# Weighing two units in one run: where the loop of a field-interaction kernel turns

## The chip, the cores and the metric

One core of a Trainium2 chip runs the whole kernel. The time is that of the device for one execution, in microseconds (us); lower is better. TensorE multiplies, VectorE forms products, ScalarE copies, GpSimd (POOL) and SyncE (SP) set up and issue transfers.

## The reference

```python
def _cin_forward(x, Ws):
    x0 = x
    h = x
    outs = []
    for W in Ws:
        h = jnp.einsum('bid,bjd,ijh->bhd', x0, h, W)
        outs.append(h)
    out = jnp.concatenate(outs, axis=1)
    return out.sum(axis=-1)
```

x has 512 rows of 39 fields of 64 numbers, W0 is 39 x 39 x 128 and W1 is 39 x 128 x 128; all of it is float32. The result is 512 x 256: for each row the sums over the 64 numbers of both layers' 128 outputs. The kernel uses that the last sum runs over d: products of fields can be summed first and weighed with the (combined) weights afterwards.

## The kernel before, in words

A setup multiplies W1 by W0 into combined weights and sorts them into lists (`c0`, `c1`); it ends at about 95 us and isn't touched by the change.

After it the 512 rows are 256 pairs of rows. A **unit** is 8 pairs, a **four** is 4 of them, and a **batch** is 64 pairs, 8 units. There are 4 batches. For each unit:

- SP loads `x_w` (the windows, 360 KB, L301) and `x_d` (the listed fields, 448 KB, L308), each into one of two buffers. The order of SP's queue is x_d of unit u, then x_w of unit u, and so on. x_w of u waits until TensorE has done the sums of u-2; x_d of u waits until products and singles of u-2 are done.
- VectorE forms the unit's products in one of two buffers (L413 to L422), after the sums of unit u-2 have read it. ScalarE adds 10 single columns to each list (`singles`, L509).
- TensorE sums (L614): 96 matmuls for each four, in 4-byte floats and so with two passes each where one stands in the code, 64 rows by 32 columns of weights. A four fills two PSUM banks; four banks are used in turn, so four q waits until ScalarE has emptied the banks of four q-2.
- ScalarE empties the banks (L557), two copies for a four, into the batch's slots `s0`: 115 slots of 128 x 128.

The slots of a finished batch are **weighed** during the next batch: a slot is multiplied with its weights and added to `out_ps` (L630, 26 matmul records for 13 slots). ScalarE first stages the slots, because they lie in the arena with the batch's rows spread: 13 slots for each unit, in two halves of 6 and 7 slots (L541), in one staging buffer `t_0`. Half h may be staged when half h-2 has been weighed. The last 11 slots of a batch (the rest, `REST_HALVES`) are staged and weighed after its eighth unit; then ScalarE takes the result out of PSUM (`take_out`, L532), and TensorE starts the next with `begin_out` (L625). The fourth batch is weighed at the very end in one run of 230 matmuls.

TensorE runs loops: the body of the inner one is a **turn** of two units, one for each buffer, and it turns four times in a batch. ScalarE, VectorE and SP run straight lists of instructions. Before a unit's sums TensorE's sequencer waits for windows, products and singles (L653), and before each four for its banks (L658). For weighing it waits for a staged half (L678), and calculates addresses by register instructions.

Of the kernel before, what the change touches and what calls it, by code (L numbers as in the profile page):

```python
# [28 lines left out]
LISTED = 115  # L29
SINGLES = 10  # L30
# [71 lines left out]
def cin_kernel(nc: bass.Bass, x_w: bass.AP, x_d: bass.AP, w0: bass.AP, w1: bass.AP, c1: bass.AP, out: bass.AP):  # L102
# [3 lines left out]
    PAIRS = 64  # L106
    UNIT = 8
    FOUR = 4
    BATCHES = ALL_PAIRS // PAIRS
    UNITS = ALL_PAIRS // UNIT  # L110
    FOURS = ALL_PAIRS // FOUR
    B = 2 * PAIRS
    BANK = 512
    PROD = 4 * LISTED
    PRODS, WS, DS = 2, 2, 2

    IN_BATCH = PAIRS // UNIT
    EACH = PAIRED // IN_BATCH
    HALVES = [(0, EACH // 2), (EACH // 2, EACH)]
    REST = LISTED - IN_BATCH * EACH  # L120
    REST_HALVES = [(0, EACH // 2), (EACH // 2, REST)]
# [4 lines left out]
    with ctx:  # L126
        def sem(name):
            return ctx.enter_context(nc.semaphore(name))
# [10 lines left out]
        def view(start, *dims, rows=(0, P)):  # L139

            ap = [[WORDS, rows[1] - rows[0]]] + [[step, count] for step, count in dims]
            return bass.AP(arena, rows[0] * WORDS + start, ap)

        c0 = take(PAIRED * HID)
        s0 = [take(LISTED * B)]
# [3 lines left out]
        t_0 = take(EACH * B)  # L149
# [15 lines left out]
        banks = [ctx.enter_context(nc.psum_tensor(f"stage{i}", [P, BANK], F32)) for i in range(6)]  # L165
# [14 lines left out]
        filled = sem("filled")  # L180
        emptied = sem("emptied")
# [4 lines left out]
        staged = sem("staged")  # L186
        weighed = sem("weighed")
# [10 lines left out]
        SETUP_BANKS = Y_BANKS + len(TURNS)  # L198
# [6 lines left out]
        def emptied_through_four(q):  # L205
            return SETUP_BANKS + 2 * (q + 1)
# [297 lines left out]
        @block_.scalar  # L504
        def _(act):
            def singles(u):

                act.wait_ge(d_loaded[u % DS], 16 * (u // DS + 1))
                nc.scalar.copy(view(prod0 + u % PRODS * UNIT * PROD, (PROD, UNIT), (LISTED, 4), (1, SINGLES)),  # L509
                               view(d_0 + u % DS * UNIT * D_WORDS + D_SINGLES, (D_WORDS, UNIT), (SINGLES, 4), (1, SINGLES)))\  # L510
                    .then_inc(singles_ready, 1)

            g = 0
            for f in range(FIELDS):
                for a, b in Y_PARTS:
                    act.wait_ge(filled, g + 1)
                    nc.scalar.copy(view(y0 + f * Y_WIDTH + a, (1, b - a)), banks[g % RING][:, 0:b - a]).then_inc(emptied, 1)  # L517
                    g += 1
            act.wait_ge(z_ready, 1)
            for u in range(PRODS):  # L520
                singles(u)
            for k, n in TURNS:
                act.wait_ge(filled, g + 1)
                nc.scalar.copy(view(c0 + k * HID, (1, n * HID)), banks[g % RING][:, 0:n * HID]).then_inc(emptied, 1)  # L524
                g += 1

            def take_out(n):

                act.wait_ge(weighed, IN_ALL * (n + 1) if n < BATCHES - 1 else IN_ALL * n + 1)
                if n >= 1:  # L530
                    act.wait_ge(out_stored, 16 * n)
                nc.scalar.copy(view(out_sb0, (1, 2 * HID)), out_ps[:, 0:2 * HID]).then_inc(out_free, 1)  # L532
                act.wait_ge(out_free, n + 2)
                act.dma_start(out[n * B:(n + 1) * B, :], view(out_sb0, (1, 2 * HID))).then_inc(out_stored, 16)

            def stage(first, a, b, half):


                if half >= 2:
                    act.wait_ge(weighed, half - 1)  # L540
                nc.scalar.copy(view(t_0 + a * B, (1, (b - a) * B)), view(first + a * B, (1, (b - a) * B)))\  # L541
                    .then_inc(staged, 1)

            IN_ALL = IN_BATCH * len(HALVES) + len(REST_HALVES)
            for q in range(FOURS):
                n, t = divmod(q * FOUR, PAIRS)
                u, v = q * FOUR // UNIT, t // UNIT
                if n >= 1 and t == 0:
                    act.wait_ge(emptied, emptied_through_four(q - 1))
                if n >= 1 and t % UNIT == 0:  # L550

                    for i, (a, b) in enumerate(HALVES):
                        half = (n - 1) * IN_ALL + v * len(HALVES) + i
                        stage(s0[(n - 1) % 2] + (SINGLES + v * EACH) * B, a, b, half)
                act.wait_ge(filled, SETUP_BANKS + q + 1)
                for s in range(2):
                    nc.scalar.copy(view(s0[n % 2] + s * PAIRS + t, (B, LISTED), (1, FOUR)),  # L557
                                   banks[2 * (q % 2) + s][:, 0:LISTED * FOUR].rearrange("p (n b) -> p n b", b=FOUR))\
                        .then_inc(emptied, 1)
                if (q + 1) * FOUR % UNIT == 0 and u + PRODS < UNITS:  # L560

                    singles(u + PRODS)
                if t == PAIRS - FOUR and n >= 1:

                    (a, b), (_, c) = REST_HALVES
                    half, s_at = n * IN_ALL - len(REST_HALVES), s0[(n - 1) % 2]
                    stage(s_at, a, b, half)
                    act.wait_ge(weighed, half)
                    nc.scalar.copy(view(t_0 + b * B, (1, (SINGLES - b) * B)), view(s_at + b * B, (1, (SINGLES - b) * B)))
                    nc.scalar.copy(view(t_0 + SINGLES * B, (1, (c - SINGLES) * B)),  # L570
                                   view(s_at + (SINGLES + IN_BATCH * EACH) * B, (1, (c - SINGLES) * B)))\
                        .then_inc(staged, 1)
                    take_out(n - 1)
            take_out(BATCHES - 1)
            act.wait_ge(out_stored, 16 * BATCHES)

        @block_.tensor
        def _(pe):
# [54 lines left out]
            def weigh_staged(v, a, b):  # L633

                for k in range(a, b):
                    done = weigh(t_0 + k * B, c0 + k * HID + v * (EACH * HID), False)
                done.then_inc(weighed, 1)
# [10 lines left out]
            def turn(w_wanted, unit_wanted, banks_wanted, behind):  # L648

                for v in range(PRODS):  # L650
                    pe.wait_ge(w_loaded[v], w_wanted)
                    pe.wait_ge(prod_ready, unit_wanted)
                    pe.wait_ge(singles_ready, unit_wanted)  # L653
                    pe.reg_add(unit_wanted, unit_wanted, 1)
                    for half in range(2):

                        pe.wait_ge(emptied, banks_wanted)
                        pe.reg_add(banks_wanted, banks_wanted, 2)  # L658
                        sum_four(v, half, half)
                    behind(v)  # L660
                pe.reg_add(w_wanted, w_wanted, 16)

            pe.wait_ge(emptied, SETUP_BANKS)
            with pe.register("w_wanted") as w_wanted, pe.register("unit_wanted") as unit_wanted, \
                    pe.register("banks_wanted") as banks_wanted, pe.register("staged_wanted") as staged_wanted, \
                    pe.register("out_wanted") as out_wanted:
                pe.reg_mov(w_wanted, 16)
                pe.reg_mov(unit_wanted, 1)
                pe.reg_mov(banks_wanted, emptied_through_four(-2))
                pe.reg_mov(staged_wanted, 1)  # L670
                pe.reg_mov(out_wanted, 1)
                with pe.Fori(0, IN_BATCH // PRODS):
                    turn(w_wanted, unit_wanted, banks_wanted, lambda v: None)
                pe.wait_ge(c1_ready, 1)

                def staged_half():
                    pe.wait_ge(staged, staged_wanted)
                    pe.reg_add(staged_wanted, staged_wanted, 1)  # L678

                with pe.Fori(1, BATCHES):  # L680

                    pe.wait_ge(out_free, out_wanted)
                    pe.reg_add(out_wanted, out_wanted, 1)
                    begin_out()
                    with pe.Fori(0, IN_BATCH, PRODS) as first:
                        def weigh_unit(v):
                            for a, b in HALVES:
                                staged_half()
                                weigh_staged(first + v, a, b)
                        turn(w_wanted, unit_wanted, banks_wanted, weigh_unit)  # L690
                    for a, b in REST_HALVES:
                        staged_half()
                        weigh_rest(t_0, t_0 + SINGLES * B, a, b).then_inc(weighed, 1)
            s_at = s0[(BATCHES - 1) % 2]
# [52 lines left out]
```

## Time and profile before

| | |
|---|---|
| Median of 3 runs | 311.08 us (310.79 to 311.68) |
| The profiled execution | 310.69 us |
| its span, first to last instruction | 308.9 us |
| TensorE matmuls busy | 259.3 us, 84% |
| VectorE busy | 208.3 us, 67% |
| ScalarE busy | 176.7 us, 57% |
| mean granted TensorE clock | 0.944 |

The span is what the views below divide up; some 1.8 us of the profiled execution lie around it. "Busy" of TensorE counts modelled, overlapping matmuls: it tells that there is work in the engine, and not that it runs at its peak. The stages are: setup to about 95 us, batch 0 without weighing from 95 to 135, batches 1 to 3 with weighing to 280, and the last weighing to 306.

### The profile page before, as it was taken

What the parts mean: (1) busy time and instruction counts of PE and PEld (TensorE: products, weight loads), DVE (VectorE), ACT (ScalarE), POOL (GpSimd) and SP (SyncE); (2) the same over time, 40 slices, a digit from 0 to 9 for tenths busy, and PEclk for the clock granted to TensorE, in tenths of its full rate; (3) what the DMA queues carried; (4) which work ended last, traced back from release to release, by engine and by line L of the source; (5) the groups of instructions that cost most, each with busy time, mean ns of one, the idle gap of its engine ahead of it and who ended that gap; (6) DMA issues with size and microseconds to landing.
All of it is one profiled execution on the core that took longest, in us unless ns stands there. A gap on an engine that the chain in (4) does not pass through costs nothing.

```text
span 308.9 us, 16634 instructions
## 1 busy us (share of the span) xinstructions
PE 259.3 (84%) x7333; PEld 224.4 (73%) x7333; DVE 208.3 (67%) x831; ACT 176.7 (57%) x327; POOL 40.6 (13%) x125
## 2 busy tenths in 40 slices
PE   1999999800895656667999999999999999999996
PEld 0555555400894545556999989999998999999996
DVE  1043499999943799997998976898994899600000
ACT  1577777600695444484777758777767777760000
POOL 9633597430000000000000000000000000000000
PEclk9999999955699778799999999999999999999999
DMA  7900000030012356562544533453543354100000
GB/s 246 420 34 0 2 3 0 5 115 0 7 55 62 130 168 183 160 182 93 180 144 133 189 109 125 120 201 108 182 141 124 108 170 154 48 0 17 2 0 17
DMA packets 10822, 31.93 MB, mean 103 GB/s; under 512 B 1200, under 2 KB 1712, under 8 KB 10672
## 3 DMA queue, kind: packets, MB, share of 16 engines
q1 hardware_dynamic: 10224, 31.15, 31.1%
q10 hardware_dynamic: 576, 0.52, 0.5%
q8 instruction: 10, 0.16, 0.2%
q14 instruction: 12, 0.10, 0.1%
HBM read 31.14 MB, written 0.52 MB: 103 GB/s over the span
## 4 chain that ended last, share of the span: by engine, by line
PE 77%; issue 10%; DVE 6%; ACT 5%; DMA 2%; SPq 0%; DVEq 0%
PE out_ps L630 35%; PE stage L614 22%; PE stage L591 17%; ACT arena L524 4%; DVE arena L422 3%; DVE arena L413 2%; DMA arena<-in_w 2%; PE stage L599 1%; PE out_ps L625 1%; ACT arena L557 1%; ACT arena L532 0%; DVE arena L419 0%; DVE arena L416 0%; SPq L292 0%; SPq L291 0%
## 5 line engine op out<-in xcount | busy, mean ns | idle before, releaser
L630 PE MATMUL out_ps<-arena 128*128 (+1 forms) x920 | 109.5, 278 | 1.3 <-issue 1.3
L630 PEld LDWEIGHTS out_ps<-arena 128*128 128x128 f32 x920 | 104.8, 192 | 5.8 <-issue 5.8
L614 PE MATMUL stage<-arena 64*32 64x115 f32 (+4 forms) x6144 | 82.9, 243 | 19.2 <-issue 11.6
L614 PEld LDWEIGHTS stage<-arena 64*32 64x32 f32 x6144 | 74.2, 110 | 25.5 <-issue 23.0
L422 DVE TENSOR_TENSOR arena<-arena 128x392 f32<-128x392 f32 (+5 forms) x288 | 90.4, 386 | 0.0
L557 ACT COPY arena<-stage 128x460 f32<-128x460 f32 x128 | 63.2, 545 | 31.4 <-PE stage L614 28.8
L413 DVE TENSOR_TENSOR arena<-arena 128x224 f32<-128x224 f32 (+1 forms) x192 | 58.2, 344 | 31.2 <-PE stage L614 31.2
L591 PE MATMUL stage<-arena 128*128 128x390 f32 x156 | 53.8, 508 | 6.8 <-DMA arena<-in_w 6.8
L541 ACT COPY arena<-arena 128x768 f32<-128x768 f32 (+1 forms) x51 | 44.8, 883 | 22.8 <-PE out_ps L630 21.8
L329 DVE TENSOR_TENSOR arena<-arena 128x294 f32<-128x294 f32 (+30 forms) x189 | 47.6, 327 | 14.6 <-ACT arena L517 14.4
L591 PEld LDWEIGHTS stage<-arena 128*128 128x128 f32 x156 | 30.6, 197 | 29.4 <-DVE arena L429 6.8
L517 ACT COPY arena<-stage 128x390 f32<-128x390 f32 x78 | 37.8, 485 | 21.3 <-PE stage L591 21.3
L241 POOL COPY arena<-arena 128x6 f32<-128x6 f32 (+21 forms) x117 | 28.4, 304 | 23.1 <-ACT arena L517 23.1
L599 PE MATMUL stage<-arena 128*128 128x128 f32 x105 | 13.9, 303 | 18.1 <-issue 18.1
L599 PEld LDWEIGHTS stage<-arena 128*128 128x128 f32 x105 | 13.7, 159 | 18.7 <-issue 18.7
L509 ACT COPY arena<-arena 128x320 f32<-128x320 f32 x32 | 15.5, 488 | 18.9 <-DVE arena L329 17.5
L532 ACT COPY arena<-out_ps 128x256 f32<-128x256 f32 x4 | 1.5, 373 | 31.4 <-PE out_ps L630 31.4
L416 DVE TENSOR_TENSOR arena<-arena 128x24 f32<-128x24 f32 x96 | 17.0, 177 | 0.0
L524 ACT COPY arena<-stage 128x512 f32<-128x512 f32 (+1 forms) x27 | 13.4, 676 | 1.4 <-PE stage L599 1.4
L419 DVE TENSOR_TENSOR arena<-arena 128x88 f32<-128x88 f32 x64 | 11.9, 227 | 0.0
L229 POOL MEMSET arena<- 128x13440 f32 x1 | 11.3, 11299 | 0.3 <-POOLq L736 0.3
L432 DVE TENSOR_TENSOR arena<-arena 128x1280 f32<-128x1280 f32 x1 | 1.5, 1493 | 9.2 <-DMA arena<-in_c 9.2
(13 smaller groups left out, 10.0 us busy)
## 6 DMA issues: line engine op xcount, KB each, us to landing
arena<-in_x_d SPq DMA_DIRECT2D x32, 448.0 KB, 3.8
arena<-in_x_w SPq DMA_DIRECT2D x32, 360.0 KB, 3.2
arena<-in_w SPq DMA_DIRECT2D x1, 1344.0 KB, 9.3
arena<-in_c SPq DMA_DIRECT2D x2, 640.0 KB, 10.9
arena<-in_w SPq DMA_DIRECT2D x2, 390.0 KB, 3.4
arena<-in_w SPq DMA_DIRECT2D x1, 768.0 KB, 6.5
out<-arena ACTq DMA_DIRECT2D x4, 128.0 KB, 1.7
arena<-in_w SPq DMA_DIRECT2D x1, 384.0 KB, 5.1
```

The costliest lines, as they stand in the source:

```text
L241: return nc.gpsimd.tensor_copy(view(to, *to_axes), view(at, *axes))
L329: return nc.vector.tensor_tensor(view(to, *to_axes), view(a, *a_axes), view(b, *b_axes), ALU.add)
L413: mult(view(at, T, (n, whole), (1, n)), view(x_at, D, (0, whole), (1, n)), view(x_at, D, (1, whole), (1, n)), ALU.mult)
L422: done = mult(view(to + column * LISTED + slot, T, (g1 - g0, x1 - x0), (1, g1 - g0)), view(d + D_AT[x] + x0, D, (1, x1 - x0), (0, g1 - g0) ...
L517: nc.scalar.copy(view(y0 + f * Y_WIDTH + a, (1, b - a)), banks[g % RING][:, 0:b - a]).then_inc(emptied, 1)
L524: nc.scalar.copy(view(c0 + k * HID, (1, n * HID)), banks[g % RING][:, 0:n * HID]).then_inc(emptied, 1)
L541: nc.scalar.copy(view(t_0 + a * B, (1, (b - a) * B)), view(first + a * B, (1, (b - a) * B)))\
L557: nc.scalar.copy(view(s0[n % 2] + s * PAIRS + t, (B, LISTED), (1, FOUR)), banks[2 * (q % 2) + s][:, 0:LISTED * FOUR].rearrange("p (n b) -> ...
L591: nc.tensor.matmul(claim(g)[:, 0:b - a], view(w1_0 + f * HID, (1, HID)), view(w0_0 + a, (1, b - a)), start=True, stop=True).then_inc(fille ...
L599: done = nc.tensor.transpose(bank[:, m * HID:(m + 1) * HID], view(z0 + (k + m) * B, (1, B)), view(ident0, (1, HID)))
L614: done = nc.tensor.matmul(banks[2 * four_place + s][WIDE * column:WIDE * (column + 1), 0:LISTED * FOUR] .rearrange("p (n b) -> p b n", b=F ...
L630: return nc.tensor.matmul(out_ps[:, 0:HID] if single else out_ps[:, HID:2 * HID], view(s_at, (1, B)), view(c_at, (1, HID)), start=False, s ...
```

## The change

In a turn, TensorE weighed 13 slots behind the sums of each of its two units. Now it weighs all 26 behind the sums of the first unit. The sums of the second unit are followed at once by the next turn's first unit, or by the rest in a batch's last turn. ScalarE's list is put in the order that belongs to it: it stages unit 0 ahead of a batch's first unit, and ahead of emptying each odd unit's banks it stages that unit and the one after it (or the rest). From batch 1 on it copies the singles of two coming units together, behind each even unit.

```diff
-                if n >= 1 and t % UNIT == 0:
-
-                    for i, (a, b) in enumerate(HALVES):
-                        half = (n - 1) * IN_ALL + v * len(HALVES) + i
-                        stage(s0[(n - 1) % 2] + (SINGLES + v * EACH) * B, a, b, half)
...
-                if (q + 1) * FOUR % UNIT == 0 and u + PRODS < UNITS:
-
-                    singles(u + PRODS)
...
+            for u in range(UNITS):
+                n, v = divmod(u, IN_BATCH)
+                if n >= 1 and v == 0:
+                    act.wait_ge(emptied, emptied_through_four(u * UNIT // FOUR - 1))
+                    stage_unit(n - 1, v)
+                if n >= 1 and v % PRODS == 1:
+
+                    stage_unit(n - 1, v)
+                    if v + 1 < IN_BATCH:
+                        stage_unit(n - 1, v + 1)
+                    else:
+                        stage_rest(n - 1)
+                for q in range(u * UNIT // FOUR, (u + 1) * UNIT // FOUR):
...
+                if n == 0 or v % PRODS == 0:
+                    if n >= 1 and u > IN_BATCH:
+                        singles(u - 1 + PRODS)
+                    if u + PRODS < UNITS:
+                        singles(u + PRODS)
+                if n >= 1 and v == IN_BATCH - 1:
                     take_out(n - 1)
...
-                    behind(v)
+                    if v == 0:
+                        behind()
...
-                        def weigh_unit(v):
-                            for a, b in HALVES:
-                                staged_half()
-                                weigh_staged(first + v, a, b)
-                        turn(w_wanted, unit_wanted, banks_wanted, weigh_unit)
+                        def weigh_units():
+                            for v in range(PRODS):
+                                for a, b in HALVES:
+                                    staged_half()
+                                    weigh_staged(first + v, a, b)
+                        turn(w_wanted, unit_wanted, banks_wanted, weigh_units)
```

`stage_unit` and `stage_rest` hold the same copies and waits that stood in the loop before.

## Rows read from the trace of the kernel before

**Rows 1.** The page: busy time of the engines; clock in 40 slices.

```profile
PE 259.3 (84%) x7333; PEld 224.4 (73%) x7333; DVE 208.3 (67%) x831; ACT 176.7 (57%) x327; POOL 40.6 (13%) x125
...
PEclk9999999955699778799999999999999999999999
```

**Rows 2.** Chain of waits: start us, us, what; one unit and the final weighing.

```profile
191.15 2.38 PE stage L614 x118
193.53 3.10 PE out_ps L630 x26
...
280.69 25.70 PE out_ps L630 x230
```

**Rows 3.** Timeline of one unit: start us, us, engine, line [idle before <-releaser].

```profile
191.08 2.46 PE L614 MATMUL stage<-arena 64*32 64x49 f32 x192
191.19 0.94 ACT L541 COPY arena<-arena 128x896 f32<-128x896 f32 x1 [0.73 <-PE out_ps L630]
192.48 2.08 ACT L557 COPY arena<-stage 128x460 f32<-128x460 f32 x4 [0.36 <-PE stage L614]
...
193.47 3.17 PE L630 MATMUL out_ps<-arena 128*128 x26
193.57 0.33 SPq L301 DMA_DIRECT2D arena<-in_x_w  x1
193.65 1.22 DVE L413 TENSOR_TENSOR arena<-arena 128x224 f32<-128x224 f32 x4 [0.52 <-PE stage L614]
193.99 0.38 SPq L308 DMA_DIRECT2D arena<-in_x_d  x1
194.45 0.49 ACT L509 COPY arena<-arena 128x320 f32<-128x320 f32 x1
...
195.11 0.83 ACT L541 COPY arena<-arena 128x768 f32<-128x768 f32 x1 [0.17 <-PE out_ps L630]
...
196.56 2.21 PEld L614 LDWEIGHTS stage<-arena 64*32 64x32 f32 x192
```

**Rows 4.** Timeline of batch 0's first turn, two blocks of sums in a row.

```profile
95.25 2.95 PE L614 MATMUL stage<-arena 64*32 64x49 f32 x210 [2.62 <-ACT arena L524]
96.64 2.09 ACT L557 COPY arena<-stage 128x460 f32<-128x460 f32 x4 [2.27 <-PE stage L614]
97.73 0.29 PEld L614 LDWEIGHTS stage<-arena 64*32 64x32 f32 x18 [0.27 <-issue]
...
105.04 1.11 PEld L614 LDWEIGHTS stage<-arena 64*32 64x32 f32 x63 [0.49 <-issue]
```

**Rows 5.** Sequencer's records (PEldq) from 193.1 to 195.6: ns, start us.

```profile
L678 PEldq FUSED_REGOPS  x2: 60/67/74, 193.1 to 193.9; - x2
...
L661 PEldq FUSED_REGOPS  x1: 42/42/42, 194.8 to 194.8; - x1
...
L685 PEldq COMPARE_BRANCH  x1: 215/215/215, 194.9 to 194.9; - x1
...
L658 PEldq ALU_OP  x1: 32/32/32, 195.5 to 195.5; - x1
```

**Rows 6.** Timeline of TensorE in batch 1's first turn.

```profile
139.57 2.27 PE L630 MATMUL out_ps<-arena 128*128 x18 [1.34 <-issue]
...
141.77 1.37 PE L614 MATMUL stage<-arena 64*32 64x49 f32 x104
...
144.72 1.28 PE L614 MATMUL stage<-arena 64*32 64x66 f32 x88 [1.57 <-issue]
```

**Rows 7.** DMA queues (packets, MB, share) in 140.6:142.3, 142.3:142.4 and 146:178.9.

```profile
q1 hardware_dynamic: 126, 0.40, 66.8%
...
q8 instruction: 1, 0.02, 57.6%
...
q1 hardware_dynamic: 1728, 4.97, 46.5%
```

**Rows 8.** All 32 transfers of x_d: us from issue to landing.

```profile
DMA to landing us min/median/max: 3.2/3.8/4.9
```

More of the change, by code:

```diff
@@ L544, in _ @@
             IN_ALL = IN_BATCH * len(HALVES) + len(REST_HALVES)
[L545 to L549, printed above, removed]
-                if n >= 1 and t % UNIT == 0:
-                    for i, (a, b) in enumerate(HALVES):
-                        half = (n - 1) * IN_ALL + v * len(HALVES) + i
-                        stage(s0[(n - 1) % 2] + (SINGLES + v * EACH) * B, a, b, half)
[L555 to L559, printed above, removed]
-                if (q + 1) * FOUR % UNIT == 0 and u + PRODS < UNITS:
-                    singles(u + PRODS)
[L563 to L572, printed above, removed]
@@ new lines, in stage_unit, with stage_rest @@
+            def stage_unit(n, v):
+                for i, (a, b) in enumerate(HALVES):
+                    stage(s0[n % 2] + (SINGLES + v * EACH) * B, a, b, n * IN_ALL + v * len(HALVES) + i)
+            def stage_rest(n):
+                (a, b), (_, c) = REST_HALVES
+                half, s_at = (n + 1) * IN_ALL - len(REST_HALVES), s0[n % 2]
+                stage(s_at, a, b, half)
+                act.wait_ge(weighed, half)
+                nc.scalar.copy(view(t_0 + b * B, (1, (SINGLES - b) * B)), view(s_at + b * B, (1, (SINGLES - b) * B)))
+                nc.scalar.copy(view(t_0 + SINGLES * B, (1, (c - SINGLES) * B)),
+                               view(s_at + (SINGLES + IN_BATCH * EACH) * B, (1, (c - SINGLES) * B))).then_inc(staged, 1)
@@ new lines, in _ @@
+            for u in range(UNITS):
[10 more added lines that the diff above has]
+                for q in range(u * UNIT // FOUR, (u + 1) * UNIT // FOUR):
+                    t = q * FOUR % PAIRS
+                    act.wait_ge(filled, SETUP_BANKS + q + 1)
+                    for s in range(2):
+                        nc.scalar.copy(view(s0[n % 2] + s * PAIRS + t, (B, LISTED), (1, FOUR)),
+                                       banks[2 * (q % 2) + s][:, 0:LISTED * FOUR].rearrange("p (n b) -> p n b", b=FOUR))\
+                            .then_inc(emptied, 1)
+                if n == 0 or v % PRODS == 0:
[4 more added lines that the diff above has]
+                if n >= 1 and v == IN_BATCH - 1:
@@ L672, in _ @@
                 with pe.Fori(0, IN_BATCH // PRODS):
-                    turn(w_wanted, unit_wanted, banks_wanted, lambda v: None)
+                    turn(w_wanted, unit_wanted, banks_wanted, lambda: None)
                 pe.wait_ge(c1_ready, 1)
```

## Prediction

> **What bounds the kernel now.** I read the page first, then the chain of waits, then the timeline of one steady turn, and last the records of TensorE's sequencer. TensorE is busy in 84% of the span and every other engine is at 67% or less, and its granted clock is in the nines, at the 2.4 GHz level, from slice 17 on [rows 1]. The chain of waits shows the same from the first batch with weighing to the end: 2.38 us of sums of one unit, then 3.10 us of weighing, again and again with nothing between them [rows 2]. A unit therefore takes 5.48 us, and no other engine is waited for. What matters is only what TensorE itself loses at the seams, and who comes too late when the order changes.
>
> Two seams can be priced. The long weighing at the end runs 230 matmuls in 25.70 us, 0.1117 us each; 26 of them would take 2.905 us, but a unit's run of 26 takes 3.10 [rows 2]. So a change from sums to weighing and back costs 0.195 us inside the weighing. The rest of the seam lies inside the 2.385 us of the sums (5.48 less 3.10, rounded).
>
> **What the change does to the order.** Batches 1 to 3 have four turns each. Before, a turn is: sums of A, weigh 13 slots, sums of B, weigh 13 slots. After, it is: A, weigh 26 slots, B, and then the next turn's A. Three times in a batch B and A meet (the fourth B meets the rest of the weighing), so there are 9 such meetings in the kernel. Matmuls, copies, products and transfers keep their number. Batch 0 keeps its order.
>
> **Gain: fewer runs of weighing.** In a batch 8 runs of weighing become 5: 3 x 0.195 = 0.585 us, in three batches 1.76 us less.
>
> **Loss: B followed by A.** Two things must be done before A can start, and before the change both lie under the weighing.
> First, A's first four reuses the two banks of B's first four, which ScalarE has to empty. ScalarE starts emptying 1.40 us after the sums began (192.48 against 191.08) [rows 3]. Batch 0 already has two blocks of sums in a row: the first starts at 95.25, ScalarE empties from 96.64, and the second block's weight loads start at 97.73 and matmuls 0.03 later, 2.51 after the first block's start, with 0.27 us idle [rows 4]. Unhindered it would be about 2.21.
> Second, the loop turns between B and A. The sequencer's records tell how long this takes: it is done with a block's sums at 193.1, 2.06 us after the block's start, hardly ahead of the engine. Then it adds to a register (194.8), branches back (194.9, 215 ns), waits for windows, products and singles, and comes to the wait for the banks at 195.5 [rows 5]: 0.70 us, plus 0.03 for that wait and 0.06 until a matmul runs (a block in batch 0 starts this long after its last wait; I take the sum with 0.1 us of rounding). Today that lies under weighing already queued: the branch is at 194.9 and the queued weighing runs until 196.56. After the change nothing is queued. So A starts 2.06 + 0.70 + 0.09 = 2.85 us after B started, later than the 2.51 of the bank wait, which is thereby hidden. A second look supports it: at the one turn of batch 0's loop where nothing else is late, the weight loads pause for 0.49 us [rows 4]. The block's loads run for some 2.2 us, so this gives 2.7 at least, without the one more register move that the later loop has. The bounds for A's start are 2.51 and 2.90; I take 2.85.
> From B's start to the next weighing that makes 2.85 + 2.385 = 5.235 where two separate blocks take 4.77: 0.465 more, 9 times, 4.19 us. With the 1.76 above: net 2.43 us more. At A's start 2.51 it would be 1.13 more less 1.76, that is 0.63 less.
>
> A rule of the Trainium skill prices the branch lower: "Advanced Engine Details and Errata", Control Flow Timing, gives about 108 ns for a compare-and-branch. The record shows 215 ns for the taken one [rows 5]; by the page's figure each of the 9 meetings would be 0.11 us shorter and the total 1.0 us lower. The measured record decides.
>
> **Loss: staging for 26 slots in one run.** The staging buffer holds 13 slots in two halves. Halves 0 and 1 are staged before the weighing starts; halves 2 and 3 must be staged during it, each after the half two before it is weighed, and there is no longer a block of sums to hide this. Call the start of weighing W. ScalarE sees half 0 weighed at W + 1.64 (195.11 against 193.47) [rows 3] and needs 0.83 us. Half 1's last matmul starts at W + 2.89; ScalarE starts half 3 some 0.31 later (191.19, where that matmul had started 0.2 before the sums at 191.08) and needs 0.94: ready at W + 4.15. After it, the sequencer's wait, its address arithmetic and the weight load come: I estimate 0.27 (between 0.1, and the 0.36 from the wait's record at 193.1 to the weighing at 193.47 [rows 3, 5]). The slot is due at W + 4.35. So TensorE loses about 0.07 us in each of 12 turns, 0.84 us; from the bounds, 0 to 1.9.
> Half 2 has a second condition. In the new order ScalarE's list for a turn is: empty B's banks, empty A's banks, copy the singles of the next two units, stage half 2. The second singles copy waits for the x_d transfer of a unit two ahead, which stands in SP's queue behind the x_w load that waits for B's sums (L301, then L308) [rows 3]. So it is issued 2.91 us after B's start (193.99 against 191.08) and lands 3.8 later (3.2 to 4.9) [rows 8]: 6.7. Singles 0.40 (one copy's start to the next; its 0.49 overlaps), staging 0.83, sequencer 0.27: half 2 can be weighed at about 8.25. It is due at W + 3.0, with W = 5.235, at 8.24. So it is just in time, and every tenth that a landing is late costs a tenth. The upper half of the landings lies above 3.8; 8 turns have such a transfer; I take 0.3 us in all, 0 to 3.
> VectorE is no limit: a unit's products take 5.48 less the 0.52 idle, 4.96 us [rows 3]. It would start B's successor 2.57 after B's start, end the two units' products at 12.5, and A needs the second at about 14.2.
>
> **Gain: one wait for program code.** In batch 1's first turn TensorE stands still twice with "issue" as the only reason: before 139.57, after 8 weighing matmuls, and before 144.72, after 104 matmuls of B [rows 6]. Each follows a 0.02 MB instruction packet; the second starts between 142.3 and 142.4 and the matmuls go on 2.4 us later [rows 6, 7]. From one stop to the next the sequencer passes 18 weighing matmuls and 104 of sums, with loads 244 instructions, some 256 with its own. In the new order the same number ends in the middle of B, after about 70 matmuls. But B starts later: after 139.57 come 44 weighing matmuls, so B starts near 144.7. What held the second packet up seems to be the x_d data: in the 1.7 us before it the data queue took 66.8% of all 16 DMA engines [rows 7]. That transfer goes out when the products of unit 9 are done, which stays where it is. So the code is there at 144.7, and the second stop, 144.72 less (141.77 + some 1.17) = 1.79 us longer than a normal step, vanishes. The first stays. Bounds: 1.8 gained, or nothing if the packet comes as late relative to B as before.
>
> **Sum.** 2.43 + 0.84 + 0.3 - 1.79 = 1.8 us more. Against the profiled execution's 310.69 (span 308.9 and 1.8 around it) that is 312.5; the median of the runs shown lies 0.39 above it, so I predict 312.9.
>
> **Rivals.**
> *The code stop stays.* Then 1.79 is not gained: 314.7. For it: the packet's start may depend on how far the sequencer is in its page. Against it: the first packet was used from 139.57 on and its successor started 2.8 later, with the data queue full in between [rows 6, 7].
> *ScalarE and the x_d landing become the bound.* If landings in the new order come near 4.3 instead of 3.8, each of 8 turns loses another 0.45: 316.5. Its row reaches 4.9 [rows 8], yet x_w and x_d go out together just as now.
> *The turn of the loop is half hidden.* If A starts about 2.65 instead of 2.85 after B, 9 x 0.2 = 1.8 comes off: 311.1, no change. For it: the 0.49 us pause in batch 0 [rows 4].
> *The turn of the loop is fully hidden (faster).* The place is again between B and A: should the sequencer run far enough ahead, only the banks count, A starts at 2.51, 9 x 0.34 = 3.1 comes off and the time is 309.8. It decides from a start below 2.65 on. Against it: at 193.1 the sequencer ends the block only 0.4 before the weighing starts [rows 5], and with W 0.34 earlier the x_d landing would take back up to 0.3 in each turn.
> *Every turn of the loop fetches its code again.* Then each of 12 turns would stop for about 2.4 us with nothing queued behind the branch: up to 28 us, 340. Between 146 and 178.9, three and more turns, no packet of TensorE's instruction queue (q8) stands in the list [rows 7], so the body stays loaded. The Trainium skill has this rule in "Runtime: NRT & Kernel Launch", Instruction fetch mechanics: a branch to outside a window of two pages of 16 KiB forces a fetch. Its page also gives TensorE 128 KiB, which agrees with the trace better.
>
> **Chances.** Forecast 0.50; code stop stays 0.17; landing bound 0.08; half hidden 0.15; fully hidden 0.09; refetch 0.01. This kernel's runs differ by up to 0.3%, so a change under 0.9 us can't be told from none. Faster takes the fully hidden case, 0.09; same the half hidden one and a little of the forecast's lower edge, 0.16; slower the rest, 0.75. The range 311.2 to 315.0 holds the forecast with its bounds, the code stop and part of the half hidden case; 0.2 is left out, half of it on each side. The forecast's own range is 312.0 to 313.9.
>
> **What the new profile would show.** Pairs of blocks of sums with TensorE idle some 0.5 to 0.65 us between them, the second starting 2.85 after the first, and the chain naming issue there rather than ScalarE. Weighing runs of 52 in about 6.0 us, with a gap of under 0.1 after the 38th matmul. A turn of 11.3 us where two units take 10.96 now. In batch 1's first turn one code stop, not two. ScalarE's singles copy waiting for x_d in turns 1 to 3. VectorE idle over 1 us per turn. The prediction is wrong if A starts at 2.5, if the gap inside the 52 is over 0.3 in most turns, or if the second code stop is there.

## The result and the profile after

The changed kernel takes 312.4 us (median of 21 runs, 311.0 to 315.65) where the kernel before takes 311.08 (21 runs, 309.29 to 312.87). The ratio over all the runs is 1.007 with a 95% interval of 1.0049 to 1.0091, so the changed kernel is slower, and clear of noise. The size needs care. Six of its 21 runs lie at 314.85 to 315.65, and the other 15 around 312.3. The means (313.11 and 311.00) give 1.0068, the medians 1.0042: part of the 0.7% comes from these six runs, which the last paragraph on the prediction comes back to. The profiled execution has a span of 310.9 us and 312.72 in all.

The page of the changed kernel, busy time and clock (slices as in [rows 1]):

```profile
span 310.9 us, 16634 instructions
PE 258.9 (83%) x7333; PEld 224.4 (72%) x7333; DVE 207.4 (67%) x831; ACT 176.1 (57%) x327; POOL 40.5 (13%) x125
...
PEclk9999999955699778989999999999999999999999
```

The work is the same, and the mean granted clock is 0.945 where it was 0.944; there is no engine that got busier. The chain of waits of the changed kernel, one turn and the end:

```profile
194.06 2.39 PE stage L628 x118
196.45 0.41 issue
196.86 2.45 PE stage L628 x108
199.30 6.05 PE out_ps L644 x52
205.35 2.39 PE stage L628 x115
...
282.68 25.70 PE out_ps L644 x230
```

Against the unbroken 2.38, 3.10, 2.38, 3.10 of [rows 2] there is one piece "issue" between two blocks of sums, and a run of weighing of 6.05. A turn takes 205.35 - 194.06 = 11.29 us in this place (11.26 from the next block, at 205.28 to 216.54), where two units took 10.96. The timeline shows the same turn with the other engines:

```profile
193.99 2.46 PE L628 MATMUL stage<-arena 64*32 64x49 f32 x192
...
195.40 2.08 ACT L577 COPY arena<-stage 128x460 f32<-128x460 f32 x4 [0.36 <-PE stage L628]
...
196.82 2.23 PEld L628 LDWEIGHTS stage<-arena 64*32 64x32 f32 x192 [0.62 <-issue]
196.86 2.45 PE L628 MATMUL stage<-arena 64*32 64x49 f32 x192 [0.41 <-ACT arena L577]
...
199.23 6.12 PE L644 MATMUL out_ps<-arena 128*128 x52
...
200.21 1.01 ACT L509 COPY arena<-arena 128x320 f32<-128x320 f32 x2
201.12 0.82 ACT L541 COPY arena<-arena 128x768 f32<-128x768 f32 x1
```

A starts 196.86 - 193.99 = 2.87 us after B (2.83 in the next turn; 2.82 to 2.87 at all nine meetings). The reader should not be misled by the releaser: the line names ScalarE, L577, because that is the last semaphore that the block waited for. But those banks were empty 2.4 us after B's start. It is the sequencer's records that tell what came last, here between 196.0 and 196.9:

```profile
L676 PEldq FUSED_REGOPS  x1: 42/42/42, 196.1 to 196.1; - x1
...
L700 PEldq COMPARE_BRANCH  x1: 207/207/207, 196.2 to 196.2; - x1
...
L667 PEldq EVENT_SEMAPHORE  x1: 51/51/51, 196.5 to 196.5; - x1
...
L668 PEldq ALU_OP  x1: 36/36/36, 196.6 to 196.6; - x1
...
L672 PEldq ALU_OP  x2: 32/32/32, 195.0 to 196.8; - x2
```

The sequencer is done with B's block at 196.1, 2.1 us after B's start. It then adds to a register (L676) and branches (L700, 207 ns). The wait for windows and products comes at 196.5, that for the banks at 196.8, just before the first weight load: 0.7 us for the turn of the loop, with nothing queued. ScalarE's two singles copies follow one another without a wait for x_d here, and half 2 is staged at 201.12, in time.

The first turn of batch 1 (answers to [rows 6]):

```profile
137.65 1.16 PE L644 MATMUL out_ps<-arena 128*128 x8
140.25 5.23 PE L644 MATMUL out_ps<-arena 128*128 x44 [1.44 <-issue]
145.41 2.46 PE L628 MATMUL stage<-arena 64*32 64x49 f32 x192
148.26 2.45 PE L628 MATMUL stage<-arena 64*32 64x49 f32 x192 [0.39 <-ACT arena L577]
```

One code stop is left. B runs through its 192 matmuls without the stop of 1.57 us. The packet of code (16 KB, 0.02 MB in the list) that B needs is the only one in the instruction queue between 142.8 and 143.0:

```profile
q8 instruction: 1, 0.02, 28.8%
```

In the kernel before it started at 142.3 and B at 141.77; now it starts at 143.0 and B at 145.41.

For the comparisons below the time is cut into two stretches by TensorE's own starts: from unit 8's block of sums to unit 10's (batch 1's first turn), and from unit 10's to the last weighing (11 turns). Before they are 14.34 (134.69 to 149.03) and 131.5 us (149.03 to 280.53); after 13.00 (135.26 to 148.26) and 134.3 (148.26 to 282.52). So the change gains 1.3 us in the one and gives 2.8 away in the other. The rest of the 2.0 us between the spans, 0.6, lies ahead of unit 8, where the order of the work is the same in both; 0.5 of it is there at the first sums of batch 0 (95.75 against 95.25), so it is not an effect of the change.

### The profile page after: what moved, and what is told of

It reads as the page before. It is cut to its first block, busy times and chain, and to the rows that moved or that the text cites. A ratio compares the mean times of both kernels' runs of the same rounds, so it can differ in the third digit from the quotient of the medians.

```text
span 310.9 us, 16634 instructions
## 1 busy us (share of the span) xinstructions
PE 258.9 (83%) x7333; PEld 224.4 (72%) x7333; DVE 207.4 (67%) x831; ACT 176.1 (57%) x327; POOL 40.5 (13%) x125
## 4 chain that ended last, share of the span: by engine, by line
PE 80%; issue 11%; ACT 6%; DMA 2%; SPq 0%
PE out_ps L644 34%; PE stage L628 26%; PE stage L605 17%; ACT arena L524 4%; DMA arena<-in_w 2%; ACT arena L577 2%; PE stage L613 1%; PE out_ps L639 1%; ACT arena L532 0%; ACT arena L509 0%; SPq L292 0%; SPq L291 0%
## 5 line engine op out<-in xcount | busy, mean ns | idle before, releaser
L644 PE MATMUL out_ps<-arena 128*128 (+1 forms) x920 | 107.9, 278 | 1.4 <-issue 1.4
L577 ACT COPY arena<-stage 128x460 f32<-128x460 f32 x128 | 63.2, 545 | 33.4 <-PE stage L628 30.4
L229 POOL MEMSET arena<- 128x13440 f32 x1 | 11.3, 11297 | 0.3 <-POOLq L752 0.3
```

What stands on the lines that cost most here:

```text
L644: return nc.tensor.matmul(out_ps[:, 0:HID] if single else out_ps[:, HID:2 * HID], view(s_at, (1, B)), view(c_at, (1, HID)), start=False, s ...
```

## Experiments

All times are medians; "kernel before" is the run of it beside the experiment.

### Eight waits more at the end of the loop's body

```diff
                 pe.reg_add(w_wanted, w_wanted, 16)
+                if weighing:
+                    for done, value in ((c1_ready, 1), (ident_ready, 1), (z_ready, 1), (w0_ready, 1),
+                                        (w0_loaded, 32), (c1_loaded, 32), (z_zeroed, 1), (ident_zeroed, 1)):
+                        pe.wait_ge(done, value)
```

In the changed kernel:

> The changed kernel with 8 more waits on long-finished semaphores at the end of TensorE's loop body (batches 1 to 3); they may be packed into fewer records. Turn-of-the-loop theory: nothing covers the sequencer between B and A, so each extra record costs its own 0.1 us at each of 9 meetings; with 4 to 8 records A starts 3.2 to 3.7 us after B instead of 2.85, and the kernel is 3.5 to 7 us slower than the changed one (316 to 319 us). Rival (the meeting is bound by the banks, or by the array): no change, 312.4 us.

In the kernel before:

> The kernel before with the same 8 waits in the same place. Turn-of-the-loop theory: they lie under the weighing that is already queued (the sequencer is 1.0 us ahead at the block's last wait), so the time stays at 311.1 us within 0.3. Rival (sequencer work costs wherever it stands): 12 turns at 0.4 to 0.8 us, 316 to 320 us.

The changed kernel with it takes 320.19 us, ratio to the kernel before 1.0281 (1.0236 to 1.0326). The kernel before with it takes 311.74 beside 311.37, ratio 1.0013 (0.9991 to 1.0035), no change. The eight waits became four records. The timeline of a meeting in the changed kernel with them:

```profile
158.02 2.46 PE L628 MATMUL stage<-arena 64*32 64x49 f32 x192
161.39 2.45 PE L628 MATMUL stage<-arena 64*32 64x49 f32 x192 [0.91 <-ACT arena L577]
```

and the four records in the sequencer of the same kernel, 158 to 162:

```profile
L680 PEldq EVENT_SEMAPHORE  x4: 51/51/51, 160.2 to 160.5; - x4
```

And the chain of waits of the kernel before with the same four:

```profile
191.67 2.38 PE stage L614 x118
194.05 3.10 PE out_ps L630 x26
197.15 2.39 PE stage L614 x118
```

A starts 3.37 us after B, 0.53 later, and the idle time is again put down to ScalarE, which did nothing else than before. The start lies within the 3.2 to 3.7 expected, but the time lies above the 316 to 319. Of the 6.8 us between the two spans (317.7 and 310.9), 5.5 lie in the later stretch, which grew from 134.3 to 139.8 us (149.59 to 289.34): 8 meetings at 0.53 are 4.2, and three ends of a batch, where the rest of the weighing follows B behind the same records, are 1.5 more. Another 1.2 lie in the first turn, 0.5 for its meeting and 0.7 because the first code stop lasts 2.10 us instead of 1.44; 0.1 lies ahead of it. The medians differ by 7.8, and nothing in the two profiles explains the 1.0 beyond the spans. In the kernel before, the steady pattern doesn't move by more than a hundredth. So the added sequencer work counts here only where no matmuls are queued. The rival, that banks or the array bind the meeting, falls.

### Two steps taken out from between B and A

The additions to two registers and the wait for A's windows are made ahead of B's sums:

```diff
+                        pe.reg_add(unit_wanted, unit_wanted, 1)
+                        pe.wait_ge(w_loaded[1], w_wanted)
+                        pe.reg_add(w_wanted, w_wanted, 16)
+                        pe.wait_ge(prod_ready, unit_wanted)
+                        pe.wait_ge(singles_ready, unit_wanted)
+                        pe.reg_add(unit_wanted, unit_wanted, 1)
+                        pe.wait_ge(w_loaded[0], w_wanted)
+                        sums(1)
```

> The changed kernel with two of the sequencer's steps between B and A moved under the weighing: the addition to the windows' register and the wait for the next windows with the addition to the units' register (SP loads 11 KB more at the end for the last such wait). Turn-of-the-loop theory: each step takes 0.1 us, A starts 2.65 after B instead of 2.84, 9 x 0.19 = 1.7 us faster than the changed kernel, 310.7. Rival (banks or staging take it back): A starts 2.65 but the half-2 gap grows; 311.5 to 312.4.

The timeline of a meeting:

```profile
192.57 2.46 PE L630 MATMUL stage<-arena 64*32 64x49 f32 x192
195.30 2.44 PE L630 MATMUL stage<-arena 64*32 64x49 f32 x192 [0.27 <-ACT arena L579]
```

A starts 2.73 after B instead of 2.85: 0.12 less, where two steps at 0.1 were expected. The later stretch takes 133.4 us, 0.9 less than the changed kernel's 134.3, which is what 8 meetings at 0.12 make. So the trace shows the direction and some 60% of the size. The times don't show it: the median is 312.04 (ratio to before 1.0037, 1.0008 to 1.0065), where 310.7 was expected, and the interval overlaps that of the changed kernel's 1.007; by the medians alone the ratios are 1.0039 and 1.0042. A small part came back as gaps of some 0.04 to 0.08 at half 2, for which the next one was made.

> The changed kernel with the sequencer's steps moved early (A 2.72 after B was measured) and ScalarE's second singles copy put behind the staging of half 2. Theory (half 2 is late only through the x_d landing): the small gaps at the 26th weighing matmul, 0.04 to 0.08 us in six turns of the early one, vanish and that at the 38th is 0.05 in each turn; under 0.4 us faster than the early one, 311.7 to 312.0. Rival: other waits appear, same or slower.

It takes 311.74 (ratio 1.0031, 1.0005 to 1.0057), and its later stretch 133.3 us against 133.4. The gaps at half 2 are gone, as expected, and the 0.05 us ahead of the 39th matmul is there in every turn. So the order of the singles is worth about 0.1 us here, and the x_d landing cost no more than that. Its profile also shows something else, told at the end.

### The second code page and the x_d transfer

```diff
             def load_listed(u):
+                if u == 11:
+                    sp.wait_ge(weighed, 1)
```

> The kernel before, with SP's load of unit 11's listed fields (x_d) held until half 0 of the first weighing is done, about 140.3 us instead of 139.3. Theory (the second packet of TensorE's code is held up by this transfer's data): the packet starts near 140.7 instead of 142.3 and B of batch 1's first turn stops for under 0.5 us instead of 1.8; the kernel is 1.3 to 1.8 us faster, 309.5 us. Rival (the packet's start depends on how far the sequencer is in its page): the packet starts at 142.3 as before, no change, 311.1 us.

The instruction queue between 143.6 and 143.8, and the timeline of TensorE:

```profile
q8 instruction: 1, 0.02, 29.0%
```

```profile
141.89 1.37 PE L616 MATMUL stage<-arena 64*32 64x49 f32 x104
145.94 1.28 PE L616 MATMUL stage<-arena 64*32 64x66 f32 x88 [2.67 <-issue]
```

Neither theory nor rival came out. The packet went not to 140.7 but to 143.7, and the stop in B grew to 2.67; the kernel took 312.29 beside 311.37, ratio 1.0019 (0.9988 to 1.0049). The transfer had been moved by 1.1 us (139.3 to 140.4) and the packet by 1.4 with it: the packet follows the transfer, and I had not moved it out of the way. In the changed kernel the same edit:

> The changed kernel with the same hold. Theory: the code is there in time already, so nothing changes, 312.4 us within 0.3; the packet starts earlier in the trace. If the times near 315 that the changed kernel shows in some runs come from a late code packet in this stretch, they are gone here; if they come from elsewhere they stay in about a quarter of the runs.

311.92 us, ratio to the kernel before 1.0026 (0.9996 to 1.0056), whose interval overlaps the changed kernel's 1.0049 to 1.0091: no change that can be told. Its packet moved later, to 143.2, where an earlier one was expected, and still came in time for B at 144.9. Two of the 12 runs lie at 314.26 and 315.84, so the question about these runs is not answered.

With the wait one half later (`sp.wait_ge(weighed, 2)`):

> The kernel before, with the x_d load of unit 11 held until half 1 of the first weighing is done (about 142 us), that is until after the moment at which the second code packet could go out. The first hold only moved the transfer from 139.3 to 140.4, and the packet moved from 142.3 to 143.7 with it. Theory (the packet stands behind this transfer's data): with the transfer out of the way the packet starts near 140.7 to 141.3, the stop in B shrinks from 1.8 to under 0.8 us, and the kernel is 1 to 1.8 us faster, 309.5. Rival (the packet is asked for only when the sequencer is far enough in its page): packet at 142.3 or later, no change or slower, 311.3.

The queue between 141.2 and 141.5, and the timeline of SP (the transfer) and TensorE:

```profile
q8 instruction: 1, 0.02, 19.3%
```

```profile
141.73 0.33 SPq L310 DMA_DIRECT2D arena<-in_x_d  x1
...
143.75 1.28 PE L616 MATMUL stage<-arena 64*32 64x66 f32 x88 [0.75 <-issue]
```

Now the packet starts before the transfer, 1.0 us earlier than in the kernel before, and the stop falls from 1.57 to 0.75. TensorE's own work stands 0.15 us earlier and is otherwise the same, so the rival, that the packet waits for the sequencer to come far enough in its page, falls too. Unit 8 to unit 10 takes 13.64 us instead of 14.34; the later stretch stays at 131.5. That is 0.7 us where 1 to 1.8 were expected, and in the medians, 310.45 beside 310.83, it is within the noise (0.9991, 0.9965 to 1.0016).

### The loop cut in the middle of a weighing run

```diff
+                    sums(0)
+                    weigh_unit(0)
+                    with pe.Fori(0, IN_BATCH - PRODS, PRODS) as first:
+                        weigh_unit(first + 1)
+                        sums(1)
+                        sums(0)
+                        weigh_unit(first + 2)
+                    weigh_unit(IN_BATCH - 1)
+                    sums(1)
```

> The changed kernel's order with TensorE's loop cut elsewhere: a batch starts with A and 13 slots outside the loop, and the body is 13 slots, B, A, 13 slots, three times, so that the branch lies in the middle of a weighing run. The body of a batch grows from some 960 to some 1850 instructions. Turn-of-the-loop theory: B to A is left with three sequencer steps (2.35 us after B's start), so the bank wait decides: A starts 2.51 after B, 9 x 0.33 = 3.0 us less; ScalarE's list with its wait for x_d then takes back 0.2 to 0.35 in each of 8 turns: 310 to 312. Rival (the longer body isn't kept by the sequencer): packets of code in every batch and stops of 1 to 3 us, over 316.

> The rotated loop, and ScalarE copies the second unit's singles behind staging half 2 instead of ahead of it, so that half 2 does not wait for x_d. Theory: the gap in the middle of the weighing run falls to the 0.05 us of half 3, and the kernel is 1.5 to 2.5 us faster than the rotated one, 308.5 to 309.5, below the kernel before. Rival (staging was not late in the rotated one): same as the rotated one.

340.02 us (ratio 1.0944, 1.0908 to 1.098) and 337.94 (1.0875, 1.083 to 1.0919). From the first one's page, the instruction queue, and from its timeline TensorE in batch 2, where the changed kernel has no such stops:

```profile
q8 instruction: 32, 0.52, 0.6%
```

```profile
205.06 1.99 PE L628 MATMUL stage<-arena 64*32 64x58 f32 x126 [0.30 <-issue]
208.78 1.76 PE L628 MATMUL stage<-arena 64*32 64x66 f32 x127 [1.74 <-issue]
```

32 instruction packets instead of 10, and stops in every batch: the rival, and far more than the 310 to 312 of the theory. Counted from the code, some 1850 instructions in a batch's loop are not kept, some 960 are. The Trainium skill, "Runtime: NRT & Kernel Launch", Instruction fetch mechanics, gives TensorE 2048 instructions in pages of 256, first in, first out; both loops are below this, yet the longer one is fetched anew. That could agree with it only if pages partly used and the one fetched ahead count too, which no run here shows. The section's other rule, that only two pages are held, does not hold for TensorE here: two pages would be 512 instructions, and the shorter loop of some 960 turns without a further packet. The second of these two kernels can't tell anything on the singles, and neither says where A starts after B, since the code stops cover both.

### Weighing behind the second unit, with four and with six banks

A cheaper way to bring the branch under the weighing: A, B, 26 slots, branch. ScalarE stages in the order that belongs to it.

```diff
-                    if v == 0:
+                    if v == PRODS - 1:
                         behind()
```

> Both units' slots are weighed behind the SECOND unit's sums of a turn (A, B, 26 slots, branch), with ScalarE's list ordered to match and its singles copy behind the staging of halves 2 and 3. The two blocks of sums meet inside the body and the branch lies under queued weighing. Turn-of-the-loop theory: B starts 2.51 after A (bank wait, 2.2 + 0.3 idle) instead of 2.84, and a turn without a code stop takes 2.51 + 2.385 + 6.05 = 10.95 us instead of 11.25. Against that the first turn of batch 1 meets its second page of code in the middle of B with no weighing queued: some 2.5 us more there. In all about 312 to 313.5 us. Rival (two blocks of sums in a row cost the same wherever the branch is): turn of 11.25, B 2.84 after A.

With six banks, the four fours of a turn use banks 0-1, 2-3, 4-5, 0-1, and TensorE waits for emptied banks ahead of the first and the fourth only:

```diff
+        SUM_BANKS = (0, 2, 4, 0)
...
-                        pe.wait_ge(emptied, banks_wanted)
-                        pe.reg_add(banks_wanted, banks_wanted, 2)
+                        if (v, half) == (0, 0):
+                            pe.wait_ge(emptied, banks_wanted)
+                            pe.reg_add(banks_wanted, banks_wanted, 2)
+                        if (v, half) == (1, 1):
+                            pe.wait_ge(emptied, banks_wanted)
+                            pe.reg_add(banks_wanted, banks_wanted, 6)
```

> The same, with all six staging banks used for the sums (A: 0 to 3; B: 4, 5 and 0, 1), so that B's first four needs no bank that ScalarE has yet to empty. Theory: B starts 2.3 to 2.4 after A (the sequencer's two steps), a turn takes 10.8 us, against 10.97 for two units in the kernel before, and the kernel is 1.4 to 2 us faster than with four banks: 310.5 to 312. Rival (the banks were not the limit): 2.51 and 10.95 as with four banks.

> The same with the x_d load of unit 11 held until unit 9's sums are done, so that the second page of TensorE's code is not behind it. Theory: the second stop of batch 1's first turn falls from about 3.5 to 1.9 to 2.4 us; 309.3 to 310.8, at or below the kernel before. Rival: the stop stays, or the late x_d brings a new wait: same as without the hold.

The chain of waits with four banks, then with six:

```profile
164.42 2.38 PE stage L623 x117
166.81 0.07 issue
166.87 2.45 PE stage L623 x109
169.32 6.05 PE out_ps L639 x52
175.37 2.38 PE stage L623 x118
```

```profile
164.35 4.64 PE stage L624 x226
168.99 6.05 PE out_ps L640 x52
175.04 4.64 PE stage L624 x224
```

With four banks B starts 2.52 us after A and the turn takes 10.95 us, as expected from a bank wait of 2.51: the branch was the reason for the changed kernel's 2.85. With six there is no gap at all between the blocks, the second starts 2.27 after the first, and a turn takes 10.69, better than the 10.8 expected and 0.27 less than two units before. The later stretch takes 131.3 (four banks) and 128.5 us (six) against 131.5 before and 134.3 after the change.

Yet the medians are 314.77 (ratio 1.012, 1.0081 to 1.0158; 312 to 313.5 was expected), 311.68 (1.0012, 0.9981 to 1.0042) and, with the hold, 310.32 beside 310.68 (0.9979, 0.9957 to 1.0001). The first turn gives it back: 19.5, 19.6 and 17.7 us instead of 14.34. The timeline of TensorE there, in the kernel with six banks, and under it the windows of that time (clock third from the end):

```profile
138.74 2.75 PE L624 MATMUL stage<-arena 64*32 64x49 f32 x138 [2.35 <-issue]
143.99 1.37 PE L624 MATMUL stage<-arena 64*32 64x115 f32 x54 [2.50 <-issue]
145.29 8.37 PE L640 MATMUL out_ps<-arena 128*128 x52
```

```profile
141.00:144.00 3.00, 0.50 (x23) 0.17 (x12) 2.42 (x9) 0.80 (x2) 0.00 (x0) 0.50 0.12 47
145.00:150.00 5.00, 5.00 (x37) 4.71 (x23) 4.53 (x20) 1.82 (x3) 0.00 (x0) 0.50 0.56 167
```

One stop of some 2.5 us in B was expected. What I had not counted is that the first stop is 2.35 us too, and what follows: the granted clock is at 1.2 GHz (0.50) in the two windows between 141 and 150, and the run of 52 weighing matmuls takes 8.4 us instead of 6.1. The hold shortened the turn, but not by what it was made for: the stop in B fell from 2.50 to 2.38 us only. The first stop was 1.35 in its profile, and there was less time at 1.2 GHz, with the run of 52 at 7.75; that the hold is the reason for these two is not shown. So the version beats the changed kernel with the hold, by ratios to the same kernel before of 0.9979 and 1.007, but whether it beats the kernel before stays just open.

## Why the prediction was right, and where its sizes were off

312.9 us was predicted and 312.4 measured. The forecast was 1.8 us more; the medians differ by 1.3 and the traces by 1.4 in the stretches that the change touches. That the ratio of 1.007 stands so near the forecast's 0.6% is luck: it holds the six runs near 315, for which the prediction has no term. By its steps:

- **Turn of the loop between B and A.** Predicted 2.85 us after B's start; 2.82 to 2.87 in the trace, with the bank wait hidden, and the parts are those of the prediction: 2.1 us until the sequencer is done with B, 0.7 for the turn, 0.1 until a matmul runs. That the sum fits to 0.03 is closer than parts read to 0.1 us could promise. The cause is shown from two sides: more sequencer work there costs its full length and costs nothing in the old order, and with the branch under queued weighing the start falls to the bank wait's 2.51. Of the signs, the chain names "issue" as said, the timeline does not; the matmuls are idle 0.36 to 0.41 us and the weight loads 0.59 to 0.62, where 0.5 to 0.65 was said without telling which.
- **Fewer runs of weighing.** 52 matmuls take 6.05 us; two runs of 26 took 6.20. The 0.195 for each run saved is there, less the next term.
- **Staging half 3.** Predicted 0.07 us in each turn. 6.05 is 0.05 over 52 x 0.1117 + 0.195, and it lies ahead of the 39th matmul as predicted; in 12 turns it is 0.6 instead of 0.84.
- **The x_d landing at half 2.** Predicted 0.3 us in all. The chain shows 6.13 and 6.15 instead of 6.05 in two turns only, under 0.2 us. They are the two in which ScalarE's second singles copy waits for x_d (0.19 us at 163.56, 0.22 at 260.67); that it would wait in turns 1 to 3 of each batch was wrong. Moving the singles copy brought 0.1 in the shortened version. So the condition was near to binding, as the sum said, and the size was at its low end.
- **These together.** The later stretch holds 8 meetings and 11 turns: 8 x (0.465 - 0.195) + 11 x 0.05 = 2.7 us; 2.8 were measured.
- **The code stop.** It vanished as predicted. With the 0.465 of the meeting, the 0.195 of the run saved and the 0.07 of half 3, the predicted 1.79 makes the first turn 1.45 us shorter; 1.34 was measured. The reason is in the trace: B's start moves back by 3.6 us and the packet by 0.7 only. That the packet stands behind the x_d transfer is shown by the two holds, of which the first one failed because I had the time of the request wrong. I took it that a packet is asked for 1.1 us after the last one is used; moved to 140.4 the transfer still went ahead.
- **The sum.** 1.8 us predicted, 1.4 measured from unit 8 to the last weighing (145.8 to 147.3). The 0.4 between them are for the most part half 3 (0.24 less) and the x_d landing (0.1 less).

What stays open: six of the changed kernel's 21 runs lie at 314.85 to 315.65 and none between 313.0 and that, while the highest of the kernel before is 312.87. No profile of such a run was taken. A longer code stop with the clock at 1.2 GHz behind it, shown in the last section, is worth 2.2 us; that it is at work in these runs is not shown. Their mean granted clock (0.924 to 0.946) does not set them apart from the other 15 (0.929 to 0.951). With the hold one run in 12 is above 314.85, and in the two kernels with the early steps none in 24, which is too few runs to name the reason.

## What to carry to other kernels

In this kernel, work of TensorE's sequencer (a loop's branch, register additions, waits long satisfied) was free while matmuls were queued (four records more changed nothing that can be measured) and cost its full length where none were (0.53 us at each meeting). So when an order is changed, look at what is queued when the loop turns. With the branch behind the 52 slow weighing matmuls a turn took 10.95 us, behind the quick sums 11.3. But look at the first pass through the code too: the same move made batch 1's first turn 19.5 us instead of 13.0, and the median 314.77. A gap that names another engine as releaser should be checked against the time at which that engine was done. Count the buffers of a merged block: with the branch moved, two more PSUM banks brought the second block's start from 2.52 to 2.27 us.

## What the runs showed of the hardware

- **Behind a code stop the clock can be low, and need not be.** In the version with early steps and reordered singles, the first code stop of batch 1 lasted 2.08 us instead of 1.44, and behind it the same 44 weighing matmuls took 6.81 us instead of 5.23. Timeline, and the windows behind the stop:

```profile
139.55 6.81 PE L651 MATMUL out_ps<-arena 128*128 x44 [2.08 <-issue]
```

```profile
139.60:143.40 3.80, 3.80 (x20) 3.80 (x21) 3.80 (x17) 1.32 (x3) 0.00 (x0) 0.57 0.45 125
143.60:146.20 2.60, 2.60 (x25) 2.57 (x23) 0.00 (x0) 1.46 (x2) 0.00 (x0) 1.00 0.00 0
```

  The granted clock is 0.57 on average there, that is mostly at 1.2 GHz, and 1.00 after. From unit 8 to unit 10 it takes 15.1 us where the same kernel without the reordering takes 12.9. In the changed kernel's profile the clock stayed at 1.00 behind its 1.44. A stop of the same length is no sufficient reason: in the changed kernel with eight waits more, the clock stayed at 1.00 behind one of 2.10 us, and the 44 matmuls took their 5.23:

```profile
141.04 5.23 PE L644 MATMUL out_ps<-arena 128*128 x44 [2.10 <-issue]
```

  What decides between the two is not shown.
- **An instruction packet went out behind data.** The 0.02 MB packet of TensorE's code started at 142.3, 143.7 and 141.3 us when the x_d transfer of that time was issued at 139.3, 140.4 and 141.7: in the first two cases some 3 us after it, in the third ahead of it. In the three kernels the matmuls that needed it went on 2.2 to 2.4 us after its start.
- **A taken branch of TensorE's sequencer** took 215 ns in the kernel before ([rows 5]) and 207 in the changed one. The whole turn of the loop delays the next block by 0.58 us: it starts 2.85 after the one before it, and 2.27 in the kernel with six banks, where nothing stands between them but two records of waits in the sequencer. The matmuls themselves follow each other at 0.012 us.
